# Forty-seven more products of ones on TensorE, from the first mixture's last units to the second mixture's first blocks

## The chip, the cores and the metric

One core of one Trainium2 chip runs the whole kernel. The metric is the device time of one execution in microseconds. Before the change it is 859.8 us, the median of three runs (856.44 to 868.62).

## The reference, cut to what matters

The input is 4 batch elements of 512 rows of 128 numbers, and a context of 32 rows for each element. Eight steps change x one after the other; each normalises x, computes something, and adds it scaled by tanh of a gate:

```
x = x + tanh(g_xattn[0]) * attention_with_low_rank_terms(layernorm(x), ctx)   # s = 0
x = x + tanh(g_ffn[0])   * mixture(layernorm(x))    # s = 1: 32 experts, top 8, one shared
x = x + tanh(g_xattn[1]) * attention_of_16_heads(layernorm(x), ctx, mask)     # s = 2
x = x + tanh(g_ffn[1])   * mixture(layernorm(x))    # s = 3: 8 experts, top 2
x = x + tanh(g_xattn[2]) * filter_by_fft(layernorm(x), ctx)                   # s = 4
x = x + tanh(g_ffn[2])   * mixture(layernorm(x))    # s = 5: 32 experts, top 4, one shared
x = x + tanh(g_xattn[3]) * attention(ctx, ctx, layernorm(x))                  # s = 6
x = x + tanh(g_ffn[3])   * mixture(layernorm(x))    # s = 7: 16 experts, top 2, one shared
```

The change lies between the end of s = 1 and the start of s = 3. The first mixture (s = 1) computes all experts for all rows and weighs the results. The second (s = 3) sends each row to its two experts alone.

## The kernel before, in words

The eight banks of PSUM have names: bank 0 and 1 are G, 2 and 3 are U, 4 and 5 are W, 6 is ACC, 7 is T. T is used in turns, and `use_t` waits until its last reader has freed it. `mm` (line 1238) is the helper by which every product that is no transposition is issued, so most PE rows carry that line.

`throwaway(o, n)` issues n products of a 128 by 128 tile of ones with 512 columns of ones into bank o. Nobody reads the result. The kernel before uses it at the start of the program alone (in the preparation and in front of the first projections).

**First mixture.** 4 batch elements times 17 experts (16 pairs and the shared one) make 68 units. `gu` makes the gate and up products of a unit, four units ahead. DVE, ACT and POOL turn them into a hidden tile in two parts, `h_hi` and `h_lo` (POOL, line 751, is the last). `down` then waits for `h_lo` in `wait_low` and issues three products of 512 columns into ACC. The weights of a row for a pair of experts come by DMA (`l_lo<-wd`) and DVE multiplies by them (line 2376). After the last unit, ACT copies ACC (line 977) and `out_back` turns it with four transpositions (line 1714) into T, from which DVE adds to x (line 2000).

**Second attention.** `query1(0)` makes the queries of the first element in T, ACT copies them (line 931), POOL spreads keys and values over the heads (`kbd`, `vbd`, line 758), `value1(0)` multiplies the spread values by the output weights, `xt_in(2, 1)` turns the next element's rows (line 1297). Then 16 tiles of 128 rows follow. `scores1(i)` puts a mask product and a product of queries and keys in bank i % 4, three tiles ahead of the rest; DVE subtracts the maximum (`shift1`, lines 1983 and 1984), ACT takes the exponential, DVE sums (`sums1`, lines 1990 to 1995), POOL divides (line 774), PE turns the result (`probs_t1`, line 1425), ACT copies it (line 924), and `values1` multiplies by the values into ACC, from which DVE adds to x after every fourth tile. `query1` and `value1` of the next element lie in between.

**On the way to the second mixture.** `chain1(g)` is called on every engine once per tile (g below 16) and once per block afterwards; it holds the routing of the second mixture: `rows_in1`, `logits1`, `cumulate1`, and `block_counts` in three parts on PE, the matching steps on DVE (lines 2030 to 2290), `rsqrt3` (lines 780, 782) and `dispatch` on POOL. `dispatch` (line 792) scatters rows by an indirect DMA, eight for each batch element. Elements 0 and 1 are scattered in the last tiles and right behind them. Once they have landed and the block table is there, SP loads each block's 128 rows (line 548) and its expert's weights (line 556). With g = 17 PE also prepares the filter of s = 4: four transpositions and five products of 512 columns (line 1578 and after it).

**Second mixture.** 46 blocks; the loop index is i = g - 18. `rows_t1(i)` turns the block's rows (line 1600), `up1(i - 2)` and `down1(i - 4)` are its two layers, and `chain1(g)` goes on with elements 2 and 3: `logits1(2)` with g = 18, `rows_in1(3)` with g = 19, `logits1(3)` and `cumulate1(2)` with g = 20. POOL scatters the finished blocks (`rows_back`, line 819) and elements 2 and 3 (line 792) by turns.

Of the kernel before, what the change touches and what calls it, by code (L numbers as in the profile page):

```python
# [22 lines left out]
B, S, D = 4, 512, 128  # L23
# [11 lines left out]
NC = [r + s for r, s in zip(ROUTED, SHARED)]  # L35
# [39 lines left out]
def at1(g, step):  # L75
    return g - LOOP1 == FFT1[step]
# [139 lines left out]
def build(nc, a, out, s1, s3, y3, wd, stages=8):  # L216
    with ExitStack() as ctx:
# [1010 lines left out]
        def _(pe):  # L1228
            t_uses = [0]
# [161 lines left out]
            def query1(b):  # L1391

                use_t()
                mm(T[:, :], wq1[:, :], xt[:, 0, :], True, True).then_inc(q["q1_ps"], 1)
                q1_base[b] = t_uses[0]
# [109 lines left out]
            def down(l, b, c):  # L1505
                k = knum(l, b, c)
                s = slots(l, c)[2]
                wh, wl = (wa_hi, wa_lo) if l in (0, 2) else (wb_hi, wb_lo)
                if c == 0:
                    if b or l >= 2:  # L1510
                        pe.wait_ge(q["outt_done"], fnum(l, b) - 1)
                    else:
                        pe.wait_ge(q["x_done"], x_num(2 * l, B - 1))
                if l == 2:
                    pe.wait_ge(q["h_done"], k + 1)
                    mm(ACC[:, :], wh[:, s, :].bitcast(F32), hb[:, k % 4, :], c == 0, c == NC[l] - 1).then_inc(q["down_done"], 1)
                    return
                wait_low(pe, k)
                mm(ACC[:, :], wh[:, s, :], h_hi[:, k % 3, :], c == 0, False)
                mm(ACC[:, :], wl[:, s, :], h_hi[:, k % 3, :], False, False)  # L1520
                last = mm(ACC[:, :], wh[:, s, :], h_lo[:, k % 3, :], False, c == NC[l] - 1)
                last.then_inc(q["down_done"], 1)
# [240 lines left out]
            for s in range(stages):  # L1763
                l = s // 2
                if s == 7:
                    pe.wait_ge(q["sg_done"], CB[3])
                    pe.wait_ge(q["h_done"], CB[3])
                    for g in range(SH_AT, CH_END):
                        chain(g)
                        if g in SH_UP:  # L1770
                            shared_up(SH_UP[g])
                        if g in SH_DOWN:
                            shared_down(SH_DOWN[g])
                    pe.wait_ge(q["tabi_done"], 3)
                    for i in range(NB3 + 4):
                        if i < NB3:
                            experts[i] = bounded(pe.value_load(tabi[2][0:1, i:i + 1]), E3 - 1)
                            expert_t(i)
                        if 0 <= i - 1 < NB3:
                            expert_up(i - 1)  # L1780
                        if 0 <= i - 3 < NB3:
                            hidden_t(i - 3)
                        if 0 <= i - 4 < NB3:
                            expert_down(i - 4)
                    for i in range(4 * (B - 1), 4 * B):
                        shared_up(i)
                    shared_down(B - 1)
                    continue
                if s == 0:
                    xt_in(0, 0)  # L1790
                    for j in range(3):
                        throwaway(bank[6], 2)
                        project(0, j)
                    scores0(0)
                    for i in range(16):
                        if i < 15:
                            scores0(i + 1)
                        if stages > 1:
                            if i == 7:
                                xt_in(1, 0)  # L1800
                            if i == 9:
                                logits(0, 0)
                        transpose0(i)
                        if i >= 1:
                            values0(i - 1)
                        if stages > 1 and i == 15:
                            comb_in(0, 0)
                        if i < 12:
                            if i % 4 == 0:
                                xt_in(0, i // 4 + 1)  # L1810
                            else:
                                project(i // 4 + 1, i % 4 - 1)
                    values0(15)
                elif s in (4, 6):
                    continue
                elif s == 2:
                    query1(0)
                    value1(0)
                    xt_in(2, 1)
                    scores1(0)  # L1820
                    scores1(1)
                    scores1(2)
                    for i in range(16):
                        b, k = divmod(i, TB)
                        if i + 3 < 16:
                            scores1(i + 3)
                        if i == STEP1["cum"][0]:
                            cumulate1(0)
                        probs_t1(i)
                        if b + 1 < B and k == 0:  # L1830
                            query1(b + 1)
                        if i >= 1:
                            values1(i - 1)
                        if b + 1 < B and k == 2:
                            value1(b + 1)
                        if b + 2 < B and k == 3:
                            xt_in(2, b + 2)
                        chain1(i)
                    values1(15)
                elif s == 3:  # L1840
                    for g in range(16, LOOP1 + NB1 + 5):
                        i = g - LOOP1
                        if i >= 0 and i % NP1 == 0 and i < NB1:
                            pe.wait_ge(q["tabi_done"], i // NP1 + 1)
                        if i == 0:
                            pe.wait_ge(d_wl, 16)
                        if 0 <= i < NB1:
                            experts1[i] = bounded(pe.value_load(tabi[i // NP1][0:1, i % NP1:i % NP1 + 1]), E1 - 1)
                            rows_t1(i)
                        if 0 <= i - 2 < NB1:  # L1850
                            up1(i - 2)
                        if 0 <= i - 4 < NB1:
                            down1(i - 4)
                        chain1(g)
                        if at1(g, "comb5"):
                            comb_in(2, 0)
                else:
                    def pre(b, part):
                        if part == 0:
                            xt_in(s, b)  # L1860
                        elif part == 1:
                            logits(l, b)
                        elif part == 2 and l == 2:
                            running(b)
                        elif part == 3:
                            comb_in(l, b)
                    pe.wait_ge(q["stage_used"], QBASE[l + 1])
                    if l == 2:
                        pe.wait_ge(q["shared2"], 1)
                    for c in range(AHEAD[l]):  # L1870
                        gu(l, 0, c)
                    for b in range(B):
                        for c in range(NC[l]):
                            k = b * NC[l] + c + AHEAD[l]
                            if k < B * NC[l]:
                                gu(l, *divmod(k, NC[l]))
                            down(l, b, c)
                            if b >= 1 and c == pe_back(l, b):
                                out_back(l, b - 1)
                            if l == 2:  # L1880
                                chain(b * NC[2] + c)
                            if b + 1 < B:
                                for at, p in ((PE_XN[l], 0), (PE_LOGITS[l], 1), (PE_RUN, 2), (PE_COMB[l], 3)):
                                    if c == at:
                                        pre(b + 1, p)
                            elif s == 1 and c == PE_TAIL_XT:
                                xt_in(s + 1, 0)
                            n, at = fft_steps(l, b)
                            if c == at[2]:
                                transform(n)  # L1890
                            if c == at[4]:
                                inverse(n)
                    out_back(l, B - 1)
# [796 lines left out]
```

## Time and profile before

| what | value |
|---|---|
| median of three runs | 859.8 us (856.44 to 868.62) |
| the profiled execution | 860.48 us |
| its span, first to last instruction | 858.7 us |
| PE busy | 735.1 us (86%), 3807 instructions |
| weight loads (PEld) busy | 540.6 us (63%) |
| DVE busy | 540.9 us (63%) |
| ACT busy | 342.1 us (40%) |
| POOL busy | 390.1 us (45%) |
| mean granted clock of TensorE | 0.924 |

The profile is of one execution. The span leaves out 1.8 us of the execution's own time. Busy shares are averages over eight steps with different limits; the chain of waits, followed back from the last instruction, has PE with 43%, DVE with 25%, POOL with 12% and issue with 9% of the span. In a row of the timeline the square bracket tells how long the engine was idle before, and what ended it. The granted clock is a share of full speed: 1.00 is the upper of its two levels (2.4 GHz), 0.50 the lower (1.2 GHz). The page's line of the clock shows it low around 290 us, from 365 to 390 us and around 400 us, and in a few single slices elsewhere.

### The profile page before, as it was taken

Reading aid. Unit: us, or ns where it says so; the run is one execution under the profiler, and the core shown is the slowest. Engines: PE = TensorE matmul, PEld = TensorE weight load, DVE = VectorE, ACT = ScalarE, POOL = GpSimd, SP = SyncE. Lnnn points to the kernel's source line nnn. Section 1 sums busy time; section 2 is a strip of 40 time slices with the busy share of each in tenths; the row PEclk is TensorE's granted clock in tenths of the full one; section 3 lists DMA queues with packets and bytes.
Section 4 is the critical chain, followed back from the end, with each engine's and each line's share of the span. In section 5 each row is a group of like instructions: output and inputs, shape, how many; then the busy total and the mean of one; then the engine's idle time right before and its main releaser. Section 6 shows DMA issues by size and latency. Waiting matters only on the chain.

```text
span 858.7 us, 13568 instructions
## 1 busy us (share of the span) xinstructions
PE 735.1 (86%) x3807; PEld 540.6 (63%) x3808; DVE 540.9 (63%) x1781; ACT 342.1 (40%) x770; POOL 390.1 (45%) x381
## 2 busy tenths in 40 slices
PE   6989889898989668877988887899899978888995
PEld 3467767676768445655877886565555544555663
DVE  3377878787898188863533576867687643433554
ACT  0244354545455235526544334225244433213441
POOL 2000034545456334362764344546456772244772
PEclk8899999999999699956999899999999996898999
DMA  5011649394949701024677651523227630012325
GB/s 147 9 54 50 224 155 310 112 319 149 315 139 323 214 14 30 19 94 132 177 214 214 176 149 51 158 90 110 78 86 208 193 110 11 16 36 78 102 70 147
DMA packets 100010, 113.43 MB, mean 132 GB/s; under 512 B 22137, under 2 KB 71936, under 8 KB 99810
## 3 DMA queue, kind: packets, MB, share of 16 engines
q1 hardware_dynamic: 93536, 103.33, 40.9%
q0 software_dynamic: 5024, 8.54, 2.9%
q10 hardware_dynamic: 1378, 0.69, 0.3%
q8 instruction: 33, 0.54, 0.3%
q14 instruction: 39, 0.32, 0.1%
HBM read 74.03 MB, written 40.38 MB: 133 GB/s over the span
## 4 chain that ended last, share of the span: by engine, by line
PE 43%; DVE 25%; POOL 12%; issue 9%; DMA 5%; ACT 3%; SPq 1%; ACTq 0%; POOLq 0%; DVEq 0%
PE psum L1238 39%; POOL y L819 5%; POOL hb L746 3%; DVE psum L2374 3%; DVE hb L2376 2%; POOL s L814 2%; DMA l_lo<-wd 1%; DVE hb L2367 1%; DMA wsb<-wd 1%; DVE const L1983 1%; DVE mr L2027 1%; POOL s L792 1%; DVE xn L1929 1%; POOL l_lo L780 1%; DVE stats L1916 1%
## 5 line engine op out<-in xcount | busy, mean ns | idle before, releaser
L1238 PE MATMUL psum<-xt_hi,wa_hi 128*128 128x512 f32 x272 | 127.5, 469 | 4.5 <-DVE hb L2376 2.8
L751 POOL TENSOR_TENSOR h_lo<-hb,h_hi 128x512 fp32r<-128x512 f32 x68 | 87.9, 1293 | 79.0 <-ACT h_hi L973 78.8
L819 POOL DMA_INDIRECT y<-xn x93 | 92.1, 991 | 66.1 <-DVE xn L2119 35.8
L1238 PE MATMUL psum<-xt_lo,wa_hi 128*128 128x512 f32 x272 | 108.7, 400 | 0.0
L966 ACT ACTIVATE hb<-psum 128x512 f32<-128x512 f32 x136 | 80.0, 592 | 58.6 <-PE psum L1238 57.5
L746 POOL TENSOR_TENSOR hb<-hb,wsb 128x512 f32<-128x512 f32 x64 | 82.3, 1285 | 39.8 <-DVE hb L2367 28.4
L1238 PE MATMUL psum<-hb,wa_hi 128*128 128x512 f32 x136 | 74.6, 631 | 12.8 <-POOLq L748 12.3
L723 POOL TENSOR_TENSOR rstd<-veps,neghalf 128x4 f32<-128x4 f32 x20 | 20.3, 1016 | 135.9 <-DVE veps L1921 135.4
L973 ACT ACTIVATE h_hi<-hb 128x512 fp32r<-128x512 f32 x68 | 42.9, 631 | 73.5 <-DVE hb L2376 42.2
L1238 PEld LDWEIGHTS psum<-xt_hi,wa_hi 128*128 128x128 f32 x272 | 52.4, 193 | 24.5 <-ACT hb L966 6.2
L1238 PEld LDWEIGHTS psum<-xt_lo,wa_hi 128*128 128x128 f32 x272 | 52.7, 194 | 17.0 <-issue 7.9
L1238 PE MATMUL psum<-l_lo,l_hi 128*128 (+1 forms) x204 | 58.5, 385 | 1.0 <-DVE l_hi L2316 1.0
L2367 DVE TENSOR_TENSOR hb<-hb,psum 128x512 f32<-128x512 f32 x68 | 45.0, 683 | 22.0 <-ACT hb L966 18.7
L2374 DVE TENSOR_TENSOR psum<-hb,psum 128x512 f32<-128x512 f32 x64 | 44.4, 693 | 21.3 <-PE psum L1238 15.2
L1238 PE MATMUL psum<-xt_hi,wa_lo 128*128 128x512 f32 x136 | 54.7, 402 | 0.0
L1238 PE MATMUL psum<-wpr,hb 128*128 x368 | 50.3, 282 | 0.0
L2376 DVE TENSOR_TENSOR hb<-psum,l_lo 128x512 f32<-128x512 f32 x64 | 44.2, 691 | 7.0 <-DMA l_lo<-wd 5.0
L1238 PEld LDWEIGHTS psum<-wpr,hb 128*128 128x128 f32 x368 | 46.4, 198 | 0.0
L814 POOL DMA_INDIRECT s<-l_hi,l_lo x32 | 31.7, 990 | 29.3 <-DVE l_hi L2264 12.9
L792 POOL DMA_INDIRECT s<-l_hi,l_lo x32 | 31.2, 976 | 26.9 <-DVE l_hi L2264 14.6
L1238 PEld LDWEIGHTS psum<-l_lo,l_hi 128*128 128x128 f32 x204 | 31.5, 192 | 16.2 <-issue 8.7
L1238 PE MATMUL psum<-hb 128*128 128x272 f32 (+2 forms) x96 | 35.2, 477 | 7.0 <-ACT wk L1127 4.6
(348 smaller groups left out, 1606.4 us busy)
## 6 DMA issues: line engine op xcount, KB each, us to landing
s<-l_lo SPq DMA_DIRECT2D x20, 1386.0 KB, 8.7
l_lo<-wd SPq DMA_DIRECT2D x128, 128.0 KB, 3.1
wsb<-wd SPq DMA_DIRECT2D x128, 128.0 KB, 2.9
l_hi<-in_pack SPq DMA_DIRECT2D x24, 322.0 KB, 3.4
l_lo<-in_pack SPq DMA_DIRECT2D x22, 322.0 KB, 3.6
xn<-s SPq DMA_DIRECT2D x93, 66.0 KB
stage<-in_pack SPq DMA_DIRECT2D x13, 256.0 KB, 2.6
l_lo<-in_L_ffn_routed_w SPq DMA_DIRECT2D x12, 256.0 KB, 3.9
```

Source lines behind the costliest of these rows:

```text
L723: pool.tensor_tensor(rstd[:, :], veps[:, :], neghalf[:, :], ALU.pow).then_inc(q["rstd_set"], 1)
L746: pool.tensor_tensor(hb[:, k % 4, :], hb[:, k % 4, :], wsb[:, w % 3, :], ALU.mult).then_inc(q["w_used"], 1)
L751: pool.tensor_tensor(h_lo[:, k % 3, :], hb[:, k % 4, :], h_hi[:, k % 3, :].bitcast(F32), ALU.subtract).then_inc(q["hlo_pool"], 1)
L792: pool.indirect_dma_start(s1, bass.IndirectOffsetOnAxis(idx3[:, n, i, k:k + 1], 0), xs3[i][:, TB * n + k, :], None).then_inc(d_scat1[n // ...
L814: pool.indirect_dma_start(s3, bass.IndirectOffsetOnAxis(idx3[:, n, i, k:k + 1], 0), xs3[i][:, TB * n + k, :], None).then_inc(d_scat, 16)
L819: pool.indirect_dma_start(y3, bass.IndirectOffsetOnAxis(xe3[:, j % XE, 128:129].bitcast(I32), 0), xe3[:, j % XE, 0:128], None, bounds_chec ...
L966: act.activation(hb[:, k % 4, :], G0[k % 3][:, :] if l == 0 else G[k % 2][:, :], ACT.Silu).then_inc(q["sg_done"], 1)
L973: act.activation(h_hi[:, k % 3, :], hb[:, k % 4, :], ACT.Copy).then_inc(q["hhi_done"], 1)
L1238: return pe.matmul(o, l, r, start=start, stop=stop, skip_group_check=True)
L2367: dve.tensor_tensor(h, h, U2[k % 3][:, :], ALU.mult).then_inc(q["um_done"], 1)
L2374: link(dve.tensor_tensor(u, h, u, ALU.mult))
L2376: dve.tensor_tensor(h, u, wrow[:, w % WS, :], ALU.mult).then_inc(q["h_done"], 1)
```

## The change

Products of ones are added at seven places of PE's program, 47 in all: 3 and 8 in front of the last two `down` of the first mixture, into T, behind a wait until T's last use is freed; 8 into ACC behind the first three `scores1`; 8 into bank 0 between `probs_t1(13)` and `values1(12)`; 4 into bank 0 in front of `values1(15)`; 4 into bank 0 behind `chain1(16)`; and 4 at the head of each of the first three blocks of the second mixture (bank 0 twice, then bank 1). Nothing is removed or moved on any engine.

```diff
@@ down(l, b, c)
                 wh, wl = (wa_hi, wa_lo) if l in (0, 2) else (wb_hi, wb_lo)
+                if l == 0 and k >= B * NC[0] - 2:
+                    pe.wait_ge(q["T_free"], t_uses[0])
+                    throwaway(T, 3 if c == NC[0] - 2 else 8)
                 if c == 0:
@@ s == 2
                     scores1(0)
                     scores1(1)
                     scores1(2)
+                    throwaway(ACC, 8)
                     for i in range(16):
...
                         if b + 1 < B and k == 0:
                             query1(b + 1)
+                        if i == 13:
+                            throwaway(bank[0], 8)
                         if i >= 1:
                             values1(i - 1)
...
                         chain1(i)
+                    throwaway(bank[0], 4)
                     values1(15)
@@ s == 3
                         i = g - LOOP1
+                        if 0 <= i <= 2:
+                            throwaway(bank[1 if i == 2 else 0], 4)
                         if i >= 0 and i % NP1 == 0 and i < NB1:
...
                         chain1(g)
+                        if g == 16:
+                            throwaway(bank[0], 4)
                         if at1(g, "comb5"):
```

## Rows read from the trace of the kernel before

**Rows 1.** Windows: stretch, length, busy (count) of PE, PEld, DVE, ACT, POOL, clock, DMA.
```profile
284.50:301.50 17.00, 12.21 (x28) 6.51 (x29) 2.13 (x3) 4.54 (x7) 4.31 (x4) 0.50 0.61 159
...
303.70:306.80 3.10, 0.04 (x1) 0.00 (x0) 2.89 (x8) 0.63 (x1) 1.05 (x1) 1.00 0.00 0
...
366.50:390.20 23.70, 17.83 (x75) 12.68 (x74) 11.95 (x70) 5.26 (x10) 16.60 (x18) 0.50 0.27 91
...
397.20:407.30 10.10, 7.33 (x37) 7.18 (x38) 5.58 (x43) 6.51 (x13) 1.03 (x1) 0.50 0.77 205
406.30:442.00 35.70, 30.98 (x255) 29.27 (x254) 16.19 (x84) 15.79 (x56) 27.40 (x28) 0.94 0.66 186
```

**Rows 2.** Timeline of PE at the program's start: start, length, instruction, count, idle time before.
```profile
11.05 2.74 PE L1238 MATMUL psum<-ones_bf 128*128 128x512 bf16 x6 [3.83 <-POOL xn L729]
```

**Rows 3.** Timeline of PE, the last two units and the second attention's first tiles.
```profile
282.49 0.50 PE L1238 MATMUL psum<-h_hi,wa_hi 128*128 128x512 f32 x1 [0.77 <-POOL h_lo L751]
...
286.05 0.79 PE L1238 MATMUL psum<-h_hi,wa_hi 128*128 128x512 f32 x1 [2.58 <-POOL h_lo L751]
...
306.83 0.66 PE L1425 MATMUL psum<-const,wk 128*128 128x128 f32 x4 [3.09 <-POOL wk L774]
307.33 1.02 PE L1238 MATMUL psum<-xt,const 128*128 128x512 f32 x2
```

**Rows 4.** Chain of waits, 262 to 302 us: start, length, what, count.
```profile
262.00 5.46 PE psum L1238 x24
...
286.05 1.66 PE psum L1238 x3
...
288.39 1.13 PE psum L1714 x4
...
290.40 2.09 PE psum L1238 x2
...
293.35 2.06 PE psum L1238 x8
...
296.17 1.09 PE psum L1297 x4
297.26 4.28 PE psum L1238 x6
```

**Rows 5.** Timeline of POOL at the second attention's start (values spread over heads).
```profile
291.37 1.05 POOL L758 TENSOR_TENSOR xt<-const 128x512 f32<-128x512 f32 x1
```

**Rows 6.** Timeline of DVE, second and fourth tile of the second attention.
```profile
301.56 0.69 DVE L1983 TENSOR_REDUCE const<-psum 128x16 f32<-128x512 f32 x1 [0.72 <-PE psum L1238]
...
306.96 0.69 DVE L1983 TENSOR_REDUCE const<-psum 128x16 f32<-128x512 f32 x1
```

**Rows 7.** Timeline of PE, the last tiles and the first blocks of the second mixture.
```profile
360.28 1.16 PE L1238 MATMUL psum<-xn,wk 128*128 128x128 f32 x8
...
365.10 0.46 PE L1238 MATMUL psum<-bo,ones_row 1*128 1x128 f32 x2 [2.38 <-DVE x L2000]
...
372.36 1.11 PE L1425 MATMUL psum<-const,wk 128*128 128x128 f32 x4 [0.61 <-POOL wk L774]
...
374.12 2.08 PE L1238 MATMUL psum<-xn,wk 128*128 128x128 f32 x8
...
394.31 0.33 PE L1600 MATMUL psum<-const,xn 128*128 128x128 f32 x1 [0.93 <-DMA xn<-s]
...
399.23 2.04 PE L1238 MATMUL psum<-xe1t,l_hi 128*128 128x128 f32 x8 [2.32 <-DMA l_hi<-in_pack]
401.07 1.71 PE L1238 MATMUL psum<-rw,x3t 128*128 128x8 f32 x8
```

**Rows 8.** Timeline of DVE, where it takes the counts of the first block table.
```profile
376.59 0.16 DVE L2273 TENSOR_TENSOR l_lo<-psum,moe 8x16 f32<-8x16 f32 x1 [2.61 <-PE psum L1238]
```

**Rows 9.** Timeline of POOL: the normalisation ahead of eight scatters, and element 2's first scatter.
```profile
378.65 1.04 POOL L780 TENSOR_TENSOR l_lo<-l_lo,neghalf 128x4 f32<-128x4 f32 x1 [2.66 <-DVE l_lo L1949]
...
406.26 1.03 POOL L792 DMA_INDIRECT s<-l_hi,l_lo  x1 [14.55 <-DVE l_hi L2264]
```

## The prediction, made blind

> **What bounds the kernel now.** I read the page's line of the granted clock first, then windows laid on its low places, then the chain of waits through them, and last the timelines of the engines that stand on the chain. The windows show three long stretches at the lower level that the change touches: 284.5 to 301.5, 366.5 to 390.2 and 397.2 to 407.3 us [rows 1], 50.8 us together. In none of them does PE stand still: it is busy 12.21 of 17.00, 17.83 of 23.70 and 7.33 of 10.10 us. The chain of waits is to be read with that in mind. From 286.05 us on it goes through every PE step of the second attention's opening, with DVE, ACT and POOL steps in between that do not depend on the clock [rows 4]. So this opening is serial, and what a PE step loses to the clock is lost to the end. In the second stretch POOL and DVE carry most of the chain, but at 376.59 DVE had waited 2.61 us for PE [rows 8], and at 378.65 POOL 2.66 us for DVE [rows 9]. In the third, POOL stands idle for 14.55 us until 406.26, and is then busy 27.40 of 35.70 us with indirect DMAs that follow each other [rows 9, 1]; an earlier start of that run is an earlier end.
>
> **The change, part by part.** It adds 47 products and one wait. The price of one at full clock: 24 products of 512 columns take 5.46 us, 0.23 each [rows 4]; at the lower level six products of ones take 2.74 us, 0.46 each [rows 2]. So 3, 4, 8 cost 0.7, 0.9, 1.8 us at full clock and 1.4, 1.8, 3.7 us at the lower. No row tells whether products of ones count for the clock as others do; that goes to a rival. Each addition has a cover:
> - Three in front of the last `down` but one: idle 0.77 us before it, for POOL [rows 3]. They fit, by 0.1. Eight in front of the last: idle 2.58 us [rows 3], they fit at full clock, and overrun by 1.1 at the lower. The added wait on T costs nothing: T was last used thirteen units earlier, and its reader follows within a few units; were it late, `down` and the opening behind it would wait as long.
> - Eight behind the third `scores1` push the fourth by 1.8 us. It ran right behind the third, with PE then idle for 3.09 us [rows 3]. DVE reads the fourth tile at 306.96 [rows 6], and `probs_t1(0)` starts at 306.83; the idle time holds the eight at full clock.
> - Eight before `values1(12)`: idle 2.38 us for DVE's addition to x [rows 7]; they fit.
> - Four before `values1(15)` have no cover on PE. Who waits for that step is the last addition to x, then the block table and the second normalisation for POOL, which stands behind POOL's own eight scatters of 1.03 us and their issue [rows 9]; so nothing, up to some 8 us. Four behind `chain1(16)` wait in PE's way to the table, with the same scatters as cover.
> - Twelve in the first three blocks: 2.8 us, against 0.93 us idle before the first transposition and 2.32 before `up1(0)`, which waits for its weights' DMA [rows 7]. They fit at full clock; at the lower they take 5.5 and overrun by 2.3.
>
> So at full clock the 47 cost nothing, and no DMA queue gets a new wait. What they give is the clock. The trace shows no row of this kernel with fillers at these places, so I bound each place by what the same steps take at either level.
>
> **Opening of the second attention.** At full clock: the last three `down` products 0.83 in place of 1.66 us; four transpositions 0.66 in place of 1.13 (and again 0.66 in place of 1.09 for `xt_in`); `query1` 1.02 in place of 2.09 [rows 3, 4]; `value1`, with as many columns, 1.04 less; the first two score tiles half of 4.28 [rows 4], of which I keep 1.8, the first tile's 1.07 and the 0.72 that DVE waited for the second [rows 6]. POOL limits one of these: spreading the values ends at 292.42 [rows 5] and `value1` starts at 293.35, so `query1` brings 0.85, not 1.07. Sum: 0.83 + 0.47 + 0.85 + 1.04 + 0.43 + 1.8 = 5.4 us. The lower end is 0, if the clock falls as before. I take the value in between: the fillers fill the gap of 2.58 us after which the clock was low, so the last unit, the turn back and the queries run at full clock (0.83 + 0.47 + 0.85 = 2.1). Behind them PE still waits for ACT, DVE and POOL between short steps, and nothing is added there, so I let the clock fall by `value1` and come back earlier in the scores, worth another 0.5. **2.6 us.**
>
> **Last tiles to the scatters.** Between 372.36 and the counts that DVE takes at 376.59, the transpositions (1.11), two small products and eight products (2.08) run at the lower level; at the upper the transpositions take 0.66 and the eight 1.16 [rows 3, 7], and the small ones about 0.3 less. Gain 0.45 + 0.92 + 0.3 = 1.7, within what DVE and POOL waited (2.61 and 2.66 [rows 8, 9]), so all of it passes to POOL's normalisation, its eight scatters, and the first rows of the second mixture. Lower end 0. Since PE has little to do between 369 and 372 us, where nothing is added, the clock may fall there after all; I take **1.1 us.**
>
> **First blocks.** `up1(0)` takes 2.04 at the lower level, half at the upper, and `logits1(3)` 1.71 [rows 7], so 1.0 + 0.75 = 1.75 us less until element 2's routing, DVE's slots and the start of POOL's run at 406.26. Lower end 0. Twelve fillers stand right ahead of the place where the clock fell; I take **1.3 us.**
>
> Sum 5.0 us. The profiled execution took 860.48 us (span 858.7 and 1.8 around it), 0.7 over the median of 859.8. So 860.5 - 5.0 = 855.5 us, 0.6% less than before.
>
> Here a rule of the Trainium skill bears on the sum. The rows say that the clock stayed at 1.00 over the 3.09 us in which PE did nothing for the second attention's first tile, and stayed at 0.50 through 17 us of which PE worked 12.21 [rows 1]. The page "TensorE: Matmul & The Clock Gate", section "HAM oscillation — how this bites in real kernels", holds that idle gaps between bursts of products throttle the engine again. By that rule alone the closed gaps would keep the clock up, and the sum would be 8.9 us in place of 5.0 (the first rival below); the trace agrees for the gap of 2.58 us before 286.05, not for that of 3.09.
>
> **The rivals.**
> - *The clock holds throughout.* If idle gaps alone bring it down, all three places give their upper ends: 5.4 + 1.7 + 1.75 = 8.9, so 851.6 us. For it: every idle stretch of over 2 us on PE in the rows gets fillers. Against it: 12.21 busy of 17.00 us did not lift the clock [rows 1].
> - *The clock falls where it fell.* The fillers end before the waits do, the engine then runs short steps with waits as before, and everything else is hidden: 860.5, at the median 859.8. For it: the waits at 288 to 296 us and 369 to 372 us are untouched. Against it: 8 fillers cover most of the 2.58 us. This is also how it goes if products of ones do not count for the clock.
> - *Slower: the fillers run at the lower clock ahead of real work.* Its place is every filler with a narrow cover. It decides if the clock is already low as a group of them starts; PE is in order, so they cannot be passed. Price: 1.1 in front of the last `down`, 1.6 at the fourth tile (3.7 us of fillers and 1.1 more for the tile itself, against the 3.2 us from the end of PE's work, 306.83 less the 3.09 idle, to DVE's turn at 306.96), 2.3 in the first blocks: 5.0, so 865.5 us. Against it: the last unit begins behind products at full clock, and 284.5 is later than the fillers' start.
>
> **How the numbers follow.** The forecast gets 0.50, the clock that holds 0.18, the clock that falls as before 0.20, the slower case 0.12. The predicted time is that of the likeliest: 855.5 us. The range goes from 848, the holding clock's 851.6 less what three runs of one kernel differ from their median at the low end (3.4 us), to 863, the unchanged 860.5 and somewhat over half of that; the slower case is mostly left out. The bounds of all three places lie within it. A change of 2% would be 17.2 us, about what a measurement of this kernel can tell from no change. The largest sum, 8.9 us, is half of that, and the slower one some 30% of it; only the scatter of the runs (856.44 to 868.62) could carry a case over. Faster 0.05, same 0.91, slower 0.04.
>
> **What would show each step right or wrong.** In the profile after: the clock at 1.00 past 286 us and `query1` near 1.0 us; fewer than 17 us at the lower level before the scores; the wait of 2.58 us for POOL filled, and the last `down` starting at the same time as before; DVE's 0.72 us of waiting at the second tile shorter; the fourth tile's maximum not later than the sums before it; DVE's wait for the counts under 2.61 us; POOL's second run starting earlier than 406.26 by about 5 us; `up1(0)` still waiting for its DMA. The prediction is wrong if the clock is low at the same steps, if a filler stands directly in front of a step that the chain names, or if POOL's run starts earlier and the second mixture still ends at the same time.

## The result

The change takes 854.93 us, the median of 20 runs (849.39 to 864.45), against 860.69 before (20 runs, 856.44 to 868.67). The ratio is 0.9938, with a 95% interval of 0.9915 to 0.9961: 5.3 us less, 3.4 to 7.3. (The two medians lie 5.8 us apart, within that interval.) The forecast was 855.5 us. Beside other kernels on other chips the change gave 857.00 us, a ratio of 0.9921 (0.9885 to 0.9957), and 855.55 us. (In that last series of six runs, 843.50 to 862.01 us, the comparison leaves out the three slow runs, more than 1.5% over the fastest, so its ratio, 0.9829, is not used here.)

The profiled execution after took 849.76 us with a span of 847.9, 10.8 us under the one before. This pair must not be read as the change's gain. I cut both spans at events of POOL and DVE, whose records are complete:

| stretch | before | after | difference |
|---|---|---|---|
| start to the end of the last `h_lo` on POOL | 286.00 | 281.99 | -4.01 |
| opening: to the fifth tile's maximum on DVE | 25.50 | 20.47 | -5.03 |
| loop: to the thirteenth tile's maximum | 34.95 | 34.96 | 0.01 |
| tail: to the end of element 1's scatters on POOL | 43.91 | 43.91 | 0.00 |
| blocks: to element 2's first scatter | 15.90 | 14.51 | -1.39 |
| from there to the end | 452.42 | 452.10 | -0.32 |

Four of the 10.8 us lie ahead of the opening; the after execution had fewer stretches at the lower clock in its first 280 us (a mean granted clock of 0.98 there, against 0.95). They are not to be put down to the change: a kernel that has nothing added up to that point (loop alone, below) took 280.90 us to it, and the 14 profiled executions lie between 280.90 and 288.54. The change's own part is 5.03 + 1.39 = 6.4 us here.

Windows of after answer to [rows 1] (columns as there). The opening and what leads to it are one stretch at full clock; in the tail and the blocks the clock was low three times.

```profile
278.00:302.40 24.40, 16.05 (x64) 7.87 (x64) 10.31 (x19) 8.49 (x13) 6.85 (x7) 1.00 0.55 150
358.60:368.60 10.00, 9.04 (x47) 6.84 (x48) 5.88 (x39) 1.19 (x2) 6.81 (x7) 0.50 0.12 41
368.80:375.50 6.70, 3.64 (x22) 2.14 (x21) 4.81 (x30) 2.28 (x5) 4.38 (x6) 1.00 0.47 153
375.60:382.30 6.70, 5.92 (x13) 3.24 (x14) 0.00 (x0) 2.10 (x4) 5.46 (x6) 0.50 0.28 101
...
392.70:399.40 6.70, 6.29 (x33) 6.21 (x34) 3.41 (x24) 5.12 (x12) 2.95 (x3) 0.50 0.91 258
```

The chain of waits through the opening of after, to be laid beside [rows 4]: the last `down` 0.98 in place of 1.66, the turn back 0.67 for 1.13, `value1` 1.17 for 2.06, `xt_in` 0.63 for 1.09. `query1` has left the chain: POOL's two products stand in its place.

```profile
282.04 0.98 PE psum L1238 x3
283.69 0.67 PE psum L1717 x4
284.39 0.76 DVE x L2011
285.22 1.04 POOL hb L758
286.26 1.01 POOL xt L758
287.32 1.17 PE psum L1238 x8
289.26 0.63 PE psum L1297 x4
289.89 1.09 PE psum L1238 x3
291.00 0.70 DVE const L1994
291.73 0.70 DVE wk L1995
292.52 0.70 DVE const L1994
```

PE's timeline of after, beside [rows 3]: eight products of ones in 1.91 us, 1.30 us idle left before the last `down`, and 1.86 of the 3.09 us left before `probs_t1(0)` at 297.79.

```profile
278.83 1.91 PE L1238 MATMUL psum<-ones_bf 128*128 128x512 bf16 x8
282.04 0.50 PE L1238 MATMUL psum<-h_hi,wa_hi 128*128 128x512 f32 x1 [1.30 <-POOL h_lo L751]
...
285.25 1.12 PE L1238 MATMUL psum<-xt,const 128*128 128x512 f32 x2 [0.90 <-DVEq L2664]
...
297.79 0.66 PE L1425 MATMUL psum<-const,wk 128*128 128x128 f32 x4 [1.86 <-POOL wk L774]
```

PE, DVE and POOL in the tail and the blocks of after, beside [rows 7 to 9]. The transpositions at 363.32 take 1.12 us as before, DVE waits 2.61 us for the counts as before, POOL 2.65 for 2.66. But `up1(0)` takes 1.13 in place of 2.04, behind a shorter wait for its weights, and POOL stands idle for 13.16 in place of 14.55 us ahead of element 2's first scatter.

```profile
363.32 1.12 PE L1425 MATMUL psum<-const,wk 128*128 128x128 f32 x4 [0.62 <-POOL wk L774]
...
390.43 1.13 PE L1238 MATMUL psum<-xe1t,l_hi 128*128 128x128 f32 x8 [1.36 <-DMA l_hi<-in_pack]
```

```profile
367.55 0.16 DVE L2284 TENSOR_TENSOR l_lo<-psum,moe 8x16 f32<-8x16 f32 x1 [2.61 <-PE psum L1238]
```

```profile
369.61 1.05 POOL L780 TENSOR_TENSOR l_lo<-l_lo,neghalf 128x4 f32<-128x4 f32 x1 [2.65 <-DVE l_lo L1960]
...
395.83 1.03 POOL L792 DMA_INDIRECT s<-l_hi,l_lo  x1 [13.16 <-DVE l_hi L2275]
```

### The profile page after: what moved, and what is told of

The parts are those of the page before. It is cut to its first block, busy times and chain, and to the rows that moved or that the text cites. A ratio compares the mean times of both kernels' runs of the same rounds, so it can differ in the third digit from the quotient of the medians.

```text
span 847.9 us, 13657 instructions
## 1 busy us (share of the span) xinstructions
PE 734.1 (87%) x3849; PEld 536.0 (63%) x3855; DVE 540.4 (64%) x1781; ACT 341.4 (40%) x770; POOL 390.3 (46%) x381
## 4 chain that ended last, share of the span: by engine, by line
PE 46%; DVE 28%; issue 8%; POOL 7%; DMA 5%; ACT 3%; SPq 2%; ACTq 0%; POOLq 0%; DVEq 0%
PE psum L1238 40%; DVE psum L2385 3%; POOL hb L746 2%; DVE hb L2387 2%; POOL s L814 2%; PE psum L1681 1%; DVE xn L1940 1%; DMA l_lo<-wd 1%; DVE hb L2378 1%; DVE mr L2038 1%; DVE const L1994 1%; DVE stats L1927 1%; POOL s L792 1%; DVE wk L1995 1%; POOL l_lo L780 1%
## 5 line engine op out<-in xcount | busy, mean ns | idle before, releaser
L1238 PEld LDWEIGHTS psum<-hb,wa_hi 128*128 128x128 f32 x136 | 25.1, 196 | 24.5 <-POOLq L748 18.5
```

The lines of the kernel that those rows point to most:

```text
L1238: return pe.matmul(o, l, r, start=start, stop=stop, skip_group_check=True)
```

## The experiments

Every run below has one profiled execution, cut at the same events. Since whole executions of one kernel differ by more than the change is worth, the stretches tell more than the ratios. All of them, in us:

| kernel | opening | loop | tail | blocks | ratio (95%) |
|---|---|---|---|---|---|
| before | 25.50 | 34.95 | 43.91 | 15.90 | |
| the change | 20.47 | 34.96 | 43.91 | 14.51 | 0.9938 (0.9915 to 0.9961) |
| the change, second series | 23.96 | 36.61 | 43.90 | 14.20 | 0.9921 (0.9885 to 0.9957) |
| the change, third series | 20.46 | 34.95 | 42.56 | 14.39 | |
| opening alone | 21.71 | 36.59 | 43.91 | 15.86 | 0.9980 (0.9944 to 1.0015) |
| tail alone | 25.79 | 38.56 | 43.90 | 15.84 | 0.9994 (0.9958 to 1.0030) |
| blocks alone | 25.78 | 38.49 | 43.89 | 14.31 | 0.9954 (0.9916 to 0.9992) |
| 16 columns each | 25.84 | 35.18 | 43.90 | 15.93 | 1.0010 (0.9982 to 1.0039) |
| 33 more | 21.54 | 39.65 | 42.21 | 15.76 | 0.9933 (0.9901 to 0.9965) |
| loop and tail, 34 more | 21.85 | 34.95 | 42.23 | 15.96 | 0.9951 (0.9924 to 0.9977) |
| covers filled | 20.47 | 34.95 | 42.23 | 14.18 | 0.9922 (0.9886 to 0.9958) |
| covers filled, second series | 20.46 | 34.95 | 42.21 | 14.24 | 0.9904 (0.9881 to 0.9928) |
| loop alone | 25.50 | 34.95 | 43.91 | 15.87 | 0.9968 (0.9928 to 1.0008) |
| sixteen | 20.48 | 41.21 | 43.89 | 14.18 | one run |

The theory: products of ones give time only by the clock that the steps behind them run at, and only where those steps stand on the chain. The rivals: the order of PE's program or the added wait makes the gain; or the profile of after was a lucky execution.

**Opening alone.** The change without its additions in the tail and the blocks.

> Only the 19 products of the opening (3, 8 into T, 8 into ACC). Theory from the profile after (the clock held through the whole opening): from the end of the last h_lo on POOL to the fifth tile's maximum on DVE 25.5 us before and 20.5 after; here again 20 to 21.5, and the whole kernel 0.4 to 0.6% faster (ratio 0.994 to 0.996). Rival, the forecast's own shares: 2.6 us from the opening, stretch 22.9, ratio 0.997. Rival, no part of it matters and the gain is scatter: 25.5 and a ratio of 1.00.

The opening took 21.71 us, just above the theory's range of 20 to 21.5 and 3.8 under the kernel before. The ratio, 0.998, has an interval that holds both the theory's and the rival's value; the loop of this execution was 1.6 us longer, a place with none of the 19 products of ones. The clock fell in the first score tiles here, for 3.4 us.

**Tail alone.** Only the eight before `values1(12)`, the four before `values1(15)` and the four behind `chain1(16)`.

> Only the 16 products of the last tiles (8 before values1(12), 4 before values1(15), 4 behind chain1(16)). Theory from the profile after: this place gives nothing, since the clock fell in it all the same; from the thirteenth tile's maximum (shift1(12)) to POOL's last scatter of element 1 43.9 us as before, ratio 1.00. Rival, the forecast's share: 1.1 us less in that stretch (at most 1.7), ratio 0.999. Rival, the four without cover cost: 0.9 us more.

The tail took 43.90 us: nothing gained, and nothing lost by the four without cover. The theory's value.

**Blocks alone.** Only the twelve at the heads of the first three blocks.

> Only the 12 products of the first three blocks. Theory: the clock holds or returns earlier over up1(0) and logits1(3): from POOL's last scatter of element 1 to its first of element 2 15.9 us before, 14.5 after; here 14.2 to 14.8, ratio 0.998. Rival, they stand in the way of the first rows: 16 us or more, ratio 1.000 or above.

The blocks took 14.31 us against 15.90, as the theory had it. The ratio, 0.9954, is better than the expected 0.998, which lies inside its interval.

**16 columns each.** All 47 products and the wait, but a thirty-second of the columns:

```diff
+            def short(o, n):
+                for i in range(n):
+                    mm(o[:, 0:16], ones_bf[:, :], ones_bf[:, 0:1].broadcast_to([128, 16]), True, True)
...
-                    throwaway(T, 3 if c == NC[0] - 2 else 8)
+                    short(T, 3 if c == NC[0] - 2 else 8)
```

> The change with the same 47 products at the same places and the same added wait, but of 16 columns in place of 512. Theory (it is the work on PE that keeps the clock): nothing is left of the gain; from the last h_lo to the fifth tile's maximum 25.5 us or a little more, from the last scatter of element 1 to the first of element 2 15.9, ratio 1.000. Rival (the place of the added products in the order, or the wait on T, makes the gain): opening near 20.5 to 21.7 and ratio 0.994 as with 512 columns.

No stretch is shorter than before by more than 0.01 us, and the ratio is 1.001. So neither the place in the order nor the wait does anything; it takes the time that the products keep PE at work. PE's timeline of this kernel, with the same eight products in 0.36 us, 3.33 us of idle time behind them, and `query1` at 2.07 again:

```profile
279.51 0.36 PE L1238 MATMUL psum<-ones_bf 128*128 128x16 bf16 x8
283.19 0.68 PE L1238 MATMUL psum<-h_hi,wa_hi 128*128 128x512 f32 x1 [3.33 <-POOL h_lo L751]
...
287.43 2.07 PE L1238 MATMUL psum<-xt,const 128*128 128x512 f32 x2 [0.90 <-DVEq L2669]
```

**The change once more.**

> The change itself once more, beside the others on one chip. Theory: opening 20.5 to 22, thirteenth tile to the last scatter of element 1 43.9, to the first of element 2 14.3 to 14.6, ratio 0.994. Rival (the profile of after was a lucky execution): opening 23 or more and ratio 0.997.

The opening took 23.96 us, the rival's side; tail and blocks as the theory had them, and so the ratio, 0.9921. The windows of this execution show why: the clock held through the last units and the turn back and fell as `query1` began, earlier than the forecast had let it, and again for a short time in the loop. `query1` took 2.08 and `value1` 2.04 us, as before the change.

```profile
283.60:291.20 7.60, 4.40 (x20) 2.12 (x18) 1.44 (x2) 1.23 (x2) 1.26 (x1) 1.00 0.75 192
291.30:301.40 10.10, 8.45 (x20) 4.67 (x21) 1.07 (x2) 3.16 (x4) 2.99 (x3) 0.50 0.74 208
...
318.60:321.90 3.30, 3.30 (x15) 3.02 (x14) 1.97 (x6) 0.65 (x2) 1.48 (x3) 0.50 0.02 5
```

```profile
291.27 2.08 PE L1238 MATMUL psum<-xt,const 128*128 128x512 f32 x2 [0.90 <-DVEq L2664]
...
294.21 2.04 PE L1238 MATMUL psum<-const,xt 128*128 128x128 f32 x8 [0.87 <-ACT hb L931]
```

**33 more.** Products of ones in the waits that the change leaves:

```diff
 def out_back(l, b):
+    if l == 0 and b == B - 1:
+        throwaway(bank[5], 2)
...
+                    throwaway(bank[5], 3)
                     query1(0)
+                    throwaway(bank[5], 3)
                     value1(0)
+                    throwaway(bank[5], 3)
                     xt_in(2, 1)
...
                         chain1(i)
+                        if i == 14:
+                            throwaway(bank[0], 8)
...
+                if g == TAP1:                 # head of chain1(17)
+                    throwaway(bank[0], 8)
...
+                        if i == 2:
+                            throwaway(bank[1], 6)   # before up1(0)
```

> All of the change and 33 more products of ones in the waits that it left: 2 before the last turn back, 3 each before query1(0), value1(0) and xt_in(2, 1), 8 behind chain1(14), 8 at the head of chain1(17), 6 before up1(0). Theory (each place gives up to its upper end once the clock holds): opening 20 to 20.5 us in every execution, the stretch to the last scatter of element 1 up to 1.7 us shorter than before (42.2), from there to the first scatter of element 2 at most 14.2; 7 to 9 us faster than before, ratio 0.990 to 0.992. Rival, the change already has all that is to be had: ratio 0.994 as the change. Rival, the new ones get in front of real work: slower than the change by up to 2 us (0.996).

The tail gained the 1.7 us that the working of the forecast had as its upper end (42.21). The opening missed its 20 to 20.5 (21.54): the eight in front of the last `down` ended 2.29 us before that product could start, and it ran at the lower clock. The blocks lost what the change had gained there (15.76): the second rival, in that one place. Up to `up1(0)`, which then waited for nothing, stood eight of the change's products, for the most part at the lower clock (1.36 and 1.89 us), and the six new ones (1.47). The loop took 39.65 us, the clock having fallen in it for 6.8 us and later for 3.4, with no filler near:

```profile
315.40:322.20 6.80, 6.80 (x25) 5.28 (x25) 3.12 (x8) 2.06 (x4) 3.37 (x4) 0.50 0.02 4
```

PE's timeline of this kernel at the other two places, the last `down` and `up1(0)`:

```profile
288.30 0.80 PE L1238 MATMUL psum<-h_hi,wa_hi 128*128 128x512 f32 x1 [2.29 <-POOL h_lo L751]
...
400.81 1.47 PE L1238 MATMUL psum<-ones_bf 128*128 128x512 bf16 x6
402.12 1.05 PE L1238 MATMUL psum<-xe1t,l_hi 128*128 128x128 f32 x8
```

**Loop and tail, 34 more.** The change, the two eights of the tail from the kernel above, and the loop:

```diff
+                        if i == 1:
+                            throwaway(bank[0], 6)
                         if i + 3 < 16:
                             scores1(i + 3)
...
+                        if i in (2, 6):
+                            throwaway(bank[i % 4], 6)
                         probs_t1(i)
```

> The change and 34 more: 8 behind chain1(14) and 8 at the head of chain1(17) (of the kernel with 33 more, where they brought 1.7 us), and 6 each before scores1(4), probs_t1(2) and probs_t1(6), in waits of 1.8 to 2.1 us. Theory: the tiles' loop is the place where executions differ (from the fifth tile's maximum to the thirteenth's 34.95 us where the clock held, 36.6 to 39.7 where it fell); here 35.0 to 36.6; from the thirteenth to the last scatter of element 1 42.2; to the first scatter of element 2 14.3 to 14.5; ratio 0.988 to 0.991, better than the change. Rival, the loop is bound by DVE and forgives a low clock: no gain from it, ratio 0.992. Rival, the new ones get in front of real work: the loop over 36.6 with the clock at full, ratio 0.994 or above.

Loop 34.95 and tail 42.23 as expected; blocks 15.96 and ratio 0.9951 not. PE's timeline shows where the 1.7 us went. The filter's products end sooner at full clock, the rows come by DMA when POOL's scatters have landed, so PE waits 2.40 us for them, the clock is at the lower level from the end of that wait on, and the next two groups of four products of ones take 1.87 and 1.91 us. From the first rows to `up1(0)` 6.5 us pass, with no wait, against 4.8 in after, 1.36 of them a wait for the weights:

```profile
387.12 1.03 PE L1238 MATMUL psum<-ones_bf 128*128 128x512 bf16 x4
390.56 0.47 PE L1605 MATMUL psum<-const,xn 128*128 128x128 f32 x1 [2.40 <-DMA xn<-s]
...
392.39 1.87 PE L1238 MATMUL psum<-ones_bf 128*128 128x512 bf16 x4
...
395.12 1.91 PE L1238 MATMUL psum<-ones_bf 128*128 128x512 bf16 x4
...
397.04 1.19 PE L1238 MATMUL psum<-xe1t,l_hi 128*128 128x128 f32 x8
```

**Covers filled.** The kernel above with `12 if i == 0 else 4` at the first block, 14 in place of 8 before the last `down`, and 3 each before `query1(0)`, `value1(0)` and `xt_in(2, 1)`.

> The kernel with 34 more, and three covers filled that earlier traces left open: 14 in place of 8 before the last down (16 were free there), 3 each before query1(0), value1(0) and xt_in(2, 1), and 12 in place of 4 at the head of the second mixture's first block, where 2.40 us of waiting for rows let the clock fall. Theory (what the tail gained was given back there, because the filter's products ended sooner): opening 20.5 to 21, loop 35.0, thirteenth tile to the last scatter of element 1 42.2, from there to the first scatter of element 2 at most 14.5, together 10 us less than before; ratio 0.986 to 0.990, better than the change. Rival, the fillers in front of the rows cost what they give: from the last scatter of element 1 to the first of element 2 15 or more, ratio 0.993 to 0.995.

All four stretches came out as the theory had them, 111.83 us together against 120.26 before: 8.4 less, where 10 had been expected. With twelve products in the wait for the rows, 0.65 us of it is left, the next four take 1.03 and not 1.87 us, and the blocks are back at 14.18:

```profile
385.82 2.77 PE L1238 MATMUL psum<-ones_bf 128*128 128x512 bf16 x12
389.25 0.33 PE L1605 MATMUL psum<-const,xn 128*128 128x128 f32 x1 [0.65 <-DMA xn<-s]
...
390.22 1.03 PE L1238 MATMUL psum<-ones_bf 128*128 128x512 bf16 x4
```

The ratio, 0.9922, missed the expected 0.986 to 0.990 all the same; 0.990 lies within its interval.

**Loop alone.** The kernel before and the 18 products in the loop.

> The kernel before and only the 18 products in the tiles' loop (6 each before scores1(4), probs_t1(2) and probs_t1(6)). Theory (the loop, which the change does not touch, loses 0 to 6 us to the clock from execution to execution): from the fifth tile's maximum to the thirteenth's 35.0 to 36.6 us; opening 25.5 to 25.8, thirteenth tile to the last scatter 43.9, to the first of element 2 15.9 as before; ratio 0.996 to 0.998. Rival, the loop is not helped: 36 to 39.7 and ratio 1.000.

The opening is at the lower clock as before, the loop right behind it at full clock and 34.95 us long:

```profile
279.70:296.60 16.90, 12.41 (x28) 6.67 (x29) 2.27 (x4) 4.39 (x6) 4.25 (x4) 0.50 0.59 152
306.40:341.30 34.90, 32.46 (x182) 21.87 (x180) 29.50 (x78) 18.93 (x36) 17.48 (x18) 1.00 0.18 32
```

Over all kernels the loop took 34.95 us in four of four executions with these products, and 34.95 to 41.21 in ten without (under 35 in three of them). The ratio, 0.9968, has 1 just inside its interval.

**Sixteen.** The change with 16 in place of 8 before the last `down`.

> The change with 16 in place of 8 products in front of the last down. At full clock they take 3.7 us against a wait of 2.58. Theory (PE takes them in order, and only what the wait covers is free): the last down starts about 1.1 us behind its h_lo, and from the last h_lo to DVE's addition to x 3.5 us in place of the change's 2.4. Rival (PE lets the awaited products pass): 2.4 as with 8.

From the last `h_lo` to DVE's addition 2.40 us: a miss, and no test of the order on PE, because the wait was longer here. The two last `h_lo` lay 4.32 us apart against 3.56 in the profile before, so the sixteen ended as the last came:

```profile
283.58 3.65 PE L1238 MATMUL psum<-ones_bf 128*128 128x512 bf16 x16
287.07 0.50 PE L1238 MATMUL psum<-h_hi,wa_hi 128*128 128x512 f32 x1
```

**Covers filled and the change on one chip.**

> The kernel with the covers filled once more, on one chip with the change. Theory: the same stretches (opening 20.5 to 21, loop 35.0, to the last scatter 42.2, to the first of element 2 14.2 to 14.5), ratio 0.988 to 0.992, and its median 3 to 5 us under the change's. Rival: no better than the change, medians within 2 us.

> The change beside it. Theory: opening 20.5 to 24, loop 35 to 41 as the clock falls in it, to the last scatter 43.9, to the first of element 2 14.2 to 14.5, ratio 0.992 to 0.996.

The stretches came out as expected for both, except that the change's tail took 42.56 us this time. The medians are 855.76 and 855.55 us: no better, the rival's value. The kernel with the covers filled kept within 854.71 to 856.38 us in six runs, the change within 843.50 to 862.01. Whether it is the faster on average is not shown.

## Why the prediction was right, and where its terms were off

**The sum** was 5.0 us; measured are 5.3 (3.4 to 7.3). From the executions above, with and without each group of products: opening 21.63 (three executions of the change) against 25.68 (five without), 4.0 us; tail 43.63 against 43.90 (five and five), 0.3; blocks 14.32 against 15.88 (five and five, without the kernels that add more around the blocks), 1.6. Together 5.9. That the sum comes so near is in part luck: the opening was sized 1.4 us too small and the tail 0.8 too large.

**The covers** held. The last `down` followed its `h_lo` at once, the fourth tile's maximum came right behind the sums before it (297.92 in after, with no wait), `up1(0)` still waited for its DMA, and the four before `values1(15)` cost nothing in the tail. Tail alone and 16 columns each show no cost either.

**The opening** was sized too small, 2.6 against 4.0 us. The step that failed is "I let the clock fall by `value1`": in two of three profiled executions of the change it held to the end (20.47 and 20.46), where the upper end of the working, 5.4, is nearly reached; in the third it fell earlier still, at `query1` (23.96 us), and gave 1.7. So 4.0 is a mean of unlike executions. The forecast took the gap in front of the last `down` as filled; the eight left a part of it open, and that part goes with what followed. Of six executions with eight products there, the two with the clock held had 1.30 and 1.58 us of idle time left, the three in which it fell later, at `query1` or in the scores, 1.66 to 1.68 us, and the one in which it fell at once 2.29 us (33 more). With 14 or 16 products at most 1.03 us was left, and the clock held in all three executions (20.46 to 20.48; two of them have three more each in front of `query1`, `value1` and `xt_in`). How long the gap is depends on when the last unit's row weights land, for which DVE waits (2.77 us for `l_lo<-wd` in after, 3.15 in the second series). No run varied the number alone often enough to show that this is the cause. The bound by POOL was right: its product for the values, not `query1`, stands on the chain after.

**The tail** was sized too large, 1.1 against 0.3 us. The forecast named the reason, little work between 369 and 372 us with nothing added, and still took two thirds of the upper end. The clock fell there in four of the five executions with the change's products in the tail, and the gain was 0.0; in the fifth it held longer, and the gain was 1.3. With eight more behind `chain1(14)` and eight at the head of `chain1(17)` all four executions gain 1.7.

**The blocks** were right: 1.3 forecast, 1.6 measured, and all of it passes through POOL's run, which took 31.78 us from element 2's first scatter to element 3's last before and after.

**The rivals.** The clock that holds throughout did not come, the clock that falls as before neither. The slower case did not come in the change, but its mechanism is real: in two kernels (33 more, and loop and tail) products of ones at the lower clock ahead of `up1(0)` took back 1.4 and 1.6 us of the blocks, in the first together with six at full clock.

In the kernel with loop and tail the clock was low after a wait of 2.40 us; in the kernel before it stayed at 1.00 over the 3.09 us ahead of 306.83 [rows 1]. The Trainium skill, page "TensorE: Matmul & The Clock Gate", section "HAM oscillation — how this bites in real kernels", holds that idle gaps between bursts throttle the engine, and goes by the length of the gap. By the length alone the two cannot go together: the shorter gap lost the clock and the longer one kept it, so the rule sizes no place here.

**Left open.** What sets, in one execution or another, at which step the clock falls, beyond the idle time left in the opening. The 322 to 332 us from the end of the second mixture's blocks to the end of the kernel differ by 10 us between executions, and no experiment touched them.

## What to carry to other kernels

Fill a wait with products that nobody reads only where the steps behind it are products on the chain. The safe choice is a wait longer than the products take at the lower clock; the eight in front of the last `down` were over that and paid, since the clock was still up as they started. Then read what each place gave from the stretch around it, not from the whole time. When such a filler makes PE faster, look for the next wait at once: the time saved becomes idle time in front of a DMA, the clock may fall in it, and the fillers behind it stand in the way. A gain of 0.6% under a scatter of 1.4% between runs took twenty runs of each kernel to place between 3.4 and 7.3 us; one pair of profiles showed 10.8 us here, 4.0 of them ahead of the change.

## What was not expected of the hardware

- The scatter between executions goes with the granted clock, if not strictly. Of 35 runs of the kernel before in one series the fastest took 855.63 us at a mean clock of 0.936, the slowest 869.30 at 0.914.
- The same steps run at either level in different executions. In the ten executions with nothing added to it the tiles' loop took 34.95 us at full clock and up to 41.21 where the clock fell in it; up to the last `h_lo` the profiles of before and after differ by 4.0 us, and the kernel with loop alone, which is the kernel before up to there, by 5.1.
